# Self attention with its pieces in slots: output normalisation moved, layer norm transposes apart, free places ahead of the output projection

## What is computed

```python
h = _layernorm(x, ln1_g, ln1_b)
x = x + _mha(h, h, sa_wq, sa_bq, sa_wk, sa_bk, sa_wv, sa_bv, sa_wo, sa_bo)
# _mha: q, k, v = h @ w.T + b in 16 heads of 32
#       softmax(q k^T / sqrt(32)) v, then @ wo.T + bo
```

## Time and profile before

| | us |
|---|---|
| median of 3 runs | 3602.26 (3598.32 to 3602.65) |
| the profiled execution | 3601.64 |
| its span, first to last instruction | 3599.9 |
| mean granted TensorE clock | 0.956 of full speed |
| PE busy | 3274.8 (91%) |
| DVE, ACT, POOL busy | 1747.6, 1695.5, 1279.3 |

### The profile page before, as it was taken

One profiled execution on the slowest core, in us unless ns is written; L12 is line 12 of the kernel. 1 busy time (PEld: TensorE's weight loads), 2 busy tenths in 40 slices (PEclk: granted clock), 3 DMA queues, 4 the chain that ended last, 5 costly groups with the idle time before them and its releaser, 6 DMA issues. The chain is left out here.

```text
span 3599.9 us, 44121 instructions
## 1 busy us (share of the span) xinstructions
PE 3274.8 (91%) x15024; PEld 2629.4 (73%) x15024; DVE 1747.6 (49%) x2646; ACT 1695.5 (47%) x4068; POOL 1279.3 (36%) x1424
## 2 busy tenths in 40 slices
PE   4899979999999958999999999758999799999999
PEld 3788857888888745776666667447888678888887
DVE  3566644222222136787788777535666442222221
ACT  2676644222222216666666666526766442222222
POOL 2455431111111115666666666514554211111110
PEclk8999989999999968999999999879999899999999
DMA  3112113111111132334333433231121131111110
GB/s 97 37 58 78 63 65 106 47 47 48 47 47 47 51 119 68 92 105 112 101 103 104 115 95 98 65 109 46 51 75 63 65 103 36 36 36 36 36 36 36
DMA packets 170341, 249.76 MB, mean 69 GB/s; under 512 B 38710, under 2 KB 57350, under 8 KB 170118
## 3 DMA queue, kind: packets, MB, share of 16 engines
q1 hardware_dynamic: 170118, 246.94, 22.6%
HBM read 115.45 MB, written 50.33 MB: 46 GB/s over the span
## 5 line engine op out<-in xcount | busy, mean ns | idle before, releaser
L1008 DVE TENSOR_REDUCE L1sa_nmax<-L1sa_s 128x2 f32<-128x1024 f32 x256 | 310.4, 1213 | 201.3 <-PE L1sa_s L810 201.2
L1147 POOL TENSOR_TENSOR L1sa_El<-L1sa_E,L1sa_Eh 128x1024 fp32r<-128x1024 f32 x128 | 314.6, 2458 | 163.6 <-ACT L1sa_Eh L914 126.5
L440 DVE TENSOR_TENSOR L1ff_gl<-L1ff_gf,L1ff_gh 128x512 fp32r<-128x512 f32 x128 | 95.1, 743 | 471.9 <-ACT L1ff_gh L400 471.9
L440 DVE TENSOR_TENSOR L0ff_gl<-L0ff_gf,L0ff_gh 128x512 fp32r<-128x512 f32 x128 | 95.0, 742 | 440.1 <-ACT L0ff_gh L400 440.0
L923 ACT ACTIVATE L1sa_E<-L1sa_st 128x1024 f32<-128x1024 f32 x256 | 260.5, 1018 | 87.4 <-PE L1sa_st L826 42.2
L386 ACT ACTIVATE L0ff_gf<-L0ff_f,cols 128x512 f32<-128x512 f32 x128 | 88.3, 690 | 451.4 <-PE L0ff_f L94 451.4
L386 ACT ACTIVATE L1ff_gf<-L1ff_f,cols 128x512 f32<-128x512 f32 x128 | 88.3, 690 | 450.3 <-PE L1ff_f L94 450.3
L92 PE MATMUL L1ff_f<-L1ff_hTh,L1ff_Wh 128*128 128x512 f32 x512 | 203.1, 397 | 5.7 <-POOL L1ff_hTl L235 5.7
L92 PE MATMUL L0ff_f<-L0ff_hTh,L0ff_Wh 128*128 128x512 f32 x512 | 202.9, 396 | 5.7 <-POOL L0ff_hTl L235 5.7
L914 ACT ACTIVATE L1sa_Eh<-L1sa_E 128x1024 fp32r<-128x1024 f32 x192 | 200.6, 1045 | 0.2
L92 PE MATMUL L0ff_acc<-L0ff_Wh,L0ff_gh 128*128 128x512 f32 x512 | 199.4, 389 | 1.1 <-DVE L0ff_gl L440 1.1
(11 more groups left out here) (322 smaller groups left out, 9023.6 us busy)
## 6 DMA issues: line engine op xcount, KB each, us to landing
L1sa_OLN<-L1sa_osb SPq DMA_DIRECT2D x128, 192.0 KB, 2.6
L0ff_xs<-x SPq DMA_DIRECT2D x64, 256.0 KB, 3.8
L1sa_stack_q<-L1sa_parts_q SPq DMA_DIRECT2D x128, 128.0 KB, 2.6
L1sa_stack_k<-L1sa_parts_k SPq DMA_DIRECT2D x128, 128.0 KB, 2.6
L1ff_xs<-x SPq DMA_DIRECT2D x64, 256.0 KB, 3.5
L0ca_xs<-in_x SPq DMA_DIRECT2D x32, 256.0 KB, 4.0
L0ca_stage<-in_x SPq DMA_DIRECT2D x32, 256.0 KB, 3.3
x<-L0ca_stage SPq DMA_DIRECT2D x32, 256.0 KB, 2.1
```

Of the source, the lines that this page charges most:

```text
L440: nc.vector.tensor_tensor(gl[:, j % 2, :], gf[:, j % 2, :], f32(gh[:, j % 2, :]), ALU.subtract)\
L1008: nc.vector.reduce_max(nmax[:, h % 2, 2 * (n % 2):2 * (n % 2) + 2], s_bank[:, :, :], AX.X, negate=True)\
L1147: nc.gpsimd.tensor_tensor(El[:, n % 2, :], E[:, n % 2, :], f32(Eh[:, n % 2, :]), ALU.subtract)\
```

## The change

It all stands in `self_attention` and the tables ahead of it.

- The pieces stand in 73 slots instead of 68: four free ones (None) ahead of the output projection's first unit, one behind the first T. The T pieces are no longer in a row but stand between quarters of O 2 and O 3. The 73 slots are spread over the 64 halves. The first O quarter moves from half 1 of step 3 to half 0 of step 5.
- A bank is fixed by kind: q and T have bank 0, k bank 1, V alternates, O is on 0, 1, 1, 1. `before` gives the unit ahead on the same bank.
- `o_hi` is one instruction (bias and rounding together), and moves from the start of step 8g+11 (8g+17 where g mod 4 = 0) to behind the exponential of step 8g+12 (8g+18). `o_lo` adds the bias itself, with scalar_tensor_tensor, and moves to step 8g+13 (8g+19).
- ACT: in steps with n mod 8 = 4 `o_out` comes behind `exp`. POOL: `m_split` at the start of even steps, `o_sum` one step later, `o_scaled` behind it (one step later still where g mod 4 = 1), and `place_v` in even steps only, two in some. SP: the line-up of a group's first head one step later, stacks at computed steps, loads of x three steps later. DVE: statistics of the layer norm one to three steps later.

```diff
+SA_SLOTS = (quarters("q", 0, 2) + quarters("k", 0, 2) + [None] * 4 + quarters("O", -1, 0) + quarters("O", -1, 1)
+            + quarters("q", 0, 3) + quarters("k", 0, 3) + [("T", 1, 0, 0), None] + quarters("O", -1, 2, 0, 2)
+            + [("T", 1, 1, 0)] + quarters("O", -1, 2, 2, 4) + [("T", 1, 2, 0)] + quarters("O", -1, 3, 0, 2)
+            + [("T", 1, 3, 0)] + quarters("O", -1, 3, 2, 4) + quarters("q", 1, 0) + quarters("k", 1, 0)
+            + quarters("V", 1, 0) + quarters("V", 1, 1) + quarters("q", 1, 1) + quarters("k", 1, 1)
+            + quarters("V", 1, 2) + quarters("V", 1, 3))
...
+def sa_bank(kind, i):
+    return {"q": 0, "k": 1, "T": 0}.get(kind, i % 2 if kind == "V" or i < 2 else 1)
...
+        for i, quarter in enumerate(SA_SLOTS):
+            if quarter:
+                half = i * 2 * STEPS // len(SA_SLOTS)
+                halves[half].append(quarter)
+                ready[quarter[:3]] = half // 2 + half % 2
...
+        stack_steps = sorted((max(ready[n, ahead, g] + 1, 8 * (g + 4 * ahead) + 4 * pair - 14), n == "k", pair, ahead, g)
+                             for n, ahead, g in ready if n in "qk" for pair in range(2))
...
-                    if n % 2 == 0 and n >= 2:
+                    if n % 8 == 3 and n >= 3:
+                        line_up((n - 3) // 2)
+                    elif n % 2 == 0 and n % 8 != 2 and n >= 2:
                         line_up((n - 2) // 2)
...
-                    if s in (15, 16, 17, 18) and b + 2 < B:
-                        load(b + 2, s - 15)
-                    if b > 0 and s in (7, 9, 16, 18):
-                        store(b - 1, (7, 9, 16, 18).index(s))
+                    if s in (18, 19, 20, 21) and b + 2 < B:
+                        load(b + 2, s - 18)
+                    if b > 0 and s in (8, 9, 16, 19):
+                        store(b - 1, (8, 9, 16, 19).index(s))
...
-                nc.scalar.activation(onorm[:, :], onorm[:, :], ACT.Identity, bias=badj[:, 2, g % G:g % G + 1])\
-                    .then_inc(e_ob2.sem, e_ob2.unit)
-                act.wait_ge(e_ob2.sem, e_ob2.no(g))
-                nc.scalar.activation(oTh[:, g % G, :], onorm[:, :], ACT.Copy).then_inc(e_oh.sem, e_oh.unit)
+                add_hi(nc, oTh[:, g % G, :], onorm[:, :], badj[:, 2, g % G:g % G + 1]).then_inc(e_oh.sem, e_oh.unit)
...
-                    for g in range(GROUPS):
-                        if n == 8 * g + (17 if g % G == 0 else 11):
-                            o_hi(g)
-                    if n % 2 == 0 and n >= 2:
+                    if n % 2 == 0 and n % 8 != 4 and n >= 2:
                         o_out((n - 2) // 2)
                     if 0 <= n + 1 < PAIRS and EH_BY[(n + 1) % 8] == "act":
                         e_hi(n + 1)
                     if 0 <= n + LEAD_T < PAIRS:
                         exp(n + LEAD_T)
+                    if n % 8 == 4 and n >= 4:
+                        o_out((n - 2) // 2)
+                    for g in range(GROUPS):
+                        if n == 8 * g + (18 if g % G == 0 else 12):
+                            o_hi(g)
...
-                add_lo(nc, oTl[:, g % G, :], oTh[:, g % G, :], onorm[:, :], None).then_inc(e_ol.sem, e_ol.unit)
+                add_lo(nc, oTl[:, g % G, :], oTh[:, g % G, :], onorm[:, :], badj[:, 2, g % G:g % G + 1])\
+                    .then_inc(e_ol.sem, e_ol.unit)
...
-                        if n == 8 * g + (17 if g % G == 0 else 11):
+                        if n == 8 * g + (19 if g % G == 0 else 13):
                             o_lo(g)
...
-                        if s in (25, 27, 29, 31):
-                            normalise(b + 2, (s - 25) // 2)
+                        if s in (26, 28, 30, 31):
+                            normalise(b + 2, (26, 28, 30, 31).index(s))
...
-            PLACE = {1: 0, 2: 1, 3: 2, 4: 3, 5: 4, 6: 5, 7: 6}
+            PLACE = {1: 0, 2: 2, 3: 2, 4: 4, 5: 4, 6: 6, 7: 6}
...
+                    if n % 2 == 0 and 0 <= n + 6 < PAIRS:
+                        m_split((n + 6) // 2)
                     if n % 8 == 2 and n >= 10:
-                        o_scaled((n - 10) // 8)
+                        o_sum((n - 10) // 8)
+                    for g in range(GROUPS):
+                        if n == 8 * g + (11 if g % G == 1 else 10):
+                            o_scaled(g)
                     if 0 <= n + 1 < PAIRS and EH_BY[(n + 1) % 8] == "pool":
                         e_hi(n + 1)
-                    if n % 8 == 1 and n >= 9:
-                        o_sum((n - 9) // 8)
                     if 0 <= n + 1 < PAIRS and EL_BY[(n + 1) % 8] == "pool":
                         e_lo(n + 1)
-                    if n % 2 and 0 <= n + 7 < PAIRS:
-                        m_split((n + 7) // 2)
```

More of the change, by code:

```diff
@@ L549, in _, with quarters @@
                 body(b, b % 2, b == B - 1)
[L552 to L554 removed]
+def quarters(kind, ahead, i, first=0, end=4):
+    return [(kind, ahead, i, c) for c in range(first, end)]
+SA_SLOTS = (quarters("q", 0, 2) + quarters("k", 0, 2) + [None] * 4 + quarters("O", -1, 0) + quarters("O", -1, 1)
[4 more added lines that the diff above has]
+            + quarters("V", 1, 2) + quarters("V", 1, 3))
 SA_FIRST = [("T", c) for c in range(KT)] + [("q", 0), ("k", 0)] + [("V", t) for t in range(TT)] + [("q", 1), ("k", 1)]
 STEPS = H * 2
[L559 to L565 removed]
+def sa_bank(kind, i):
+    return {"q": 0, "k": 1, "T": 0}.get(kind, i % 2 if kind == "V" or i < 2 else 1)
 def self_attention(nc, name, cst, x_in, x_biased, x_out, ln_w, ln_b, wq, bq, wk, bkv, wv, wo):
@@ L607, in self_attention @@
         LEAD_S, LEAD_T = 8, 2
-        halves = sa_pieces()
-        ready = {u[:3]: half // 2 + half % 2 for half, quarters in enumerate(halves) for u in quarters}
+        halves = [[] for _ in range(2 * STEPS)]
+        ready = {}
+        for i, quarter in enumerate(SA_SLOTS):
[3 more added lines that the diff above has]
+                ready[quarter[:3]] = half // 2 + half % 2
         evacs = [[] for _ in range(PAIRS + 1)]
@@ L612, in self_attention @@
         for b in range(B):
-            for kind, ahead, i in SA_ORDER:
+            for kind, ahead, i in dict.fromkeys(q[:3] for q in SA_SLOTS if q):
                 if exists(b + ahead):
@@ L617, in self_attention @@
         units += [("O", B - 1, t) for t in range(TT)]
-        no = {u: i for i, u in enumerate(units)}
-        product_no = {u: i for i, u in enumerate(u for u in units if u[0] != "T")}
+        before = {}
+        for bank in range(2):
+            on_bank = [u for u in units if sa_bank(u[0], u[2]) == bank]
+            before.update(zip(on_bank[1:], on_bank))
+        finished = [(kind, 0, i) for kind, i in SA_FIRST if kind != "T"]
+        for b in range(B):
+            finished += [(k, b + a, i) for k, a, i, c in filter(None, SA_SLOTS) if c == KT - 1 and exists(b + a)]
+        finished += [("O", B - 1, t) for t in range(TT)]
+        stack_steps = sorted((max(ready[n, ahead, g] + 1, 8 * (g + 4 * ahead) + 4 * pair - 14), n == "k", pair, ahead, g)
+                             for n, ahead, g in ready if n in "qk" for pair in range(2))
+        product_no = {u: i for i, u in enumerate(finished)}
         e_lnb = ph.events("lnb_set", 2)
@@ L756, in bank_free @@
             def bank_free(u):
-                kind, b, i = units[u - 2]
+                kind, b, i = before[u]
                 if kind == "T":
@@ L767, in piece @@
             def piece(kind, b, i, c):
-                u = no[kind, b, i]
-                bank = pj[u % 2]
-                if c == 0 and u >= 2:
-                    bank_free(u)
+                bank = pj[sa_bank(kind, i)]
+                if c == 0 and (kind, b, i) in before:
+                    bank_free((kind, b, i))
                 if kind == "T":
@@ L1218, in _ @@
                             place_v(b, j)
-                    if s == 23 and b + 2 < B:
+                    if s == 25 and b + 2 < B:
                         rsqrt(b + 2)
```

32 lines of the change are left out of this document (11 added, 21 removed), and 5 rows, old and new, of the table s.

## The result

| | before | after |
|---|---|---|
| median of 4 runs each on one chip, us | 3602.31 (3598.32 to 3602.65) | 3676.74 (3674.18 to 3679.47) |
| ratio | | 1.0209 (95%: 1.0192 to 1.0227) |
| span of the profiled execution | 3599.9 | 3672.4 |
| mean granted clock | 0.956 | 0.952 |

What follows compares the result with a forecast made beforehand. PE was taken to bound the kernel, busy for 91% of the span. Batches 1 to 6 (+42), batch 7 (+3), batch 0 (-5) and the end (-0.7) gave +39 on 3601.6 us: 3641 us, range 3600 to 3660.

Steps and rivals of the forecast that it cites:

- Steps 4 and 5: Around the free places: PE waits 2.1 (exponential), 0.7 (maxima's copy) and 3.0 us (oTl), together 5.8 us a batch.
- Seven waits of 0.53: Maxima's transpose in steps 2, 8, 10, 16, 18, 24, 26: 0.53 us each, 3.7 us a batch, where these had 2.1.
- T, in steps 12, 15 and 17: T pieces apart: waits of 1.3, 1.2 and 2.1 us, 4.6 a batch, where the transposes waited 4.1.
- Step 20: Transpose waits 2.6 us, as group 1's scaling in step 19 waits for group 0's low part, behind a maximum.
- rival 1: Step 5: the low part is there when PE comes to the first O piece; 3566 us, chance 0.13.
- the lock: Step 5: POOL's El blocks DVE's low part, both reading SBUF; PE waits 3.0 us, without the rule 2.0.
- the sign that I named: In the trace: oTl at 2 us and more in most cases would show the lock forecast right.
- rival 3: PE under half busy for 9 us lowers the clock longer: +2 to 4 us a batch, 3655 to 3670, chance 0.12.
- The fixed banks add nothing else, since each predecessor is over a step ahead: Banks fixed by kind: no further waits claimed, except for O2 to O3.
- costed at nothing: SP's stacks and x loads move one to three steps: no cost claimed; if cover goes, scores wait 2.6 us.
- the term of step 28: One more layer norm operation precedes a maximum in step 28: a wait of 0.4 us where 0.5 was.
- batch 0 and batch 7: Batch 0, without O, was to win 5 us (bounds 0 and -8); batch 7, without T, to lose 3.

Runs made afterwards that it cites:

- olo_first: Kernel after, with DVE making the low part (o_lo) ahead of the maximum of its step: 3634.47 us (one run).
- fused_alone: Kernel before, with only the fused o_hi and the o_lo that adds the bias, at their old places: 3611.17 us, ratio 1.0027.
- ends: Kernel after, with T in the prologue and O of the last batch alternating between the two banks again: 3673.93 us (one run).
- t3_first: Kernel after, with T3's low part ahead of the reciprocal half on DVE in step 17: 3666.37 us (one run).
- all_mended: Kernel after, with low parts and O2's sum before maxima, T3 before reciprocal, alternating end banks, pair-0 stacks first, normalisation in even steps: 3602.23 us, ratio 1.0001.
- olo_oout_sum: Kernel before, with fused o_hi, biased o_lo ahead of the maximum, o_out behind exp in every even step, o_sum one step later: 3592.98 us, ratio 0.9968.
- before_oout: Kernel before, with o_out behind the exponential on ACT in every even step: 3620.97 us, ratio 1.0056.

## Why the prediction was right or wrong

**Right: the idle time of the full batches.** Predicted were 17.1 us a batch, the trace of batch 3 has 17.6; +42 for six batches, measured +45.2. Most terms agree singly. Steps 4 and 5: 5.8 predicted, 4.7 measured (2.1, 0.7 and 3.0 against 1.48, 0.42 and 2.83). Seven waits of 0.53: six of them, 3.2 instead of 3.7. T, in steps 12, 15 and 17: 1.3, 1.2 and 2.1 predicted, 0.94, 1.01 and 1.78 measured. Step 20: 2.6 and 2.56. olo_first supports the order on DVE as the cause of the largest, and of the one in step 20, and it was the point from which rival 1 decided: the first O product waited behind a maximum of its own step. The swap removes that and gives back 42 us; on top of the fused instruction alone it gives 32. Rival 1's price doesn't follow, though. It had 3566 us for a low part that is there in time; with a wait of 0.2 us for it olo_first has 3634, since the other new waits stay.

**Right, but not as a sign: the lock.** The bounds 0.67 and a blocked low part were the right ones: fused_alone shows the new form at 2.54 us. In step 5 I reckoned POOL's El from 1.0 us into the step, and the low part from 2.3 to 3.9; the trace has 0.98, and 2.37 to 3.87. So it was held for 0.8 us of its 1.50, as forecast. But a low part of 1.6 us in the forecast's own working doesn't go with the sign that I named, oTl at 2 us and more in most cases. None of the 32 in after reaches 2 us, their mean is 1.02, and that sign failed. In the kernel before 19 of 32 are over 2 us. The wait was made by the place behind the maximum first, and by the lock second.

**Wrong: "Total +39" has no term for the clock.** Busy time grew by 14.1 us in six batches for the same products. The text had it only in the upper bound ("another 1.7 us a batch at half clock") and in rival 3. Measured are 2.3 us a batch: after the wait of step 5 the clock is at 0.50 for 6.83 us. This is the largest term that the sum lacks, 14 of the 33 us between +39 and the 72.5 of the spans. The idle time of the full batches was forecast well, and rival 3's clock came beside it, not in its place; with the other misses the time is above rival 3's 3655 to 3670 as well.

**Wrong: "The fixed banks add nothing else, since each predecessor is over a step ahead".** That was reasoned for the loop. In the prologue four T units follow each other on one bank, and at the end O1, O2 and O3 do. With the end's -0.7 for the fused instruction there should have been a gain; measured are +4.4 and +3.9, and ends gives 4.5 and 3.2 of them back.

**Wrong: SP's order, "costed at nothing".** "The first user of a stack set is some steps behind" holds for the pair issued first. The k stacks of pair 0 are issued behind q's pair 1, and the stack lands late for step 24: 1.0 us, and 0.5 in step 25. Also the term of step 28 (0.4) is 1.43 and a new 0.43 stands in step 0, both behind maxima that normalisations delay. These took 1.96 us in step 27 and 2.37 in step 30, both begun behind POOL's El, against 0.53 without it. The same section of the Trainium skill (SBUF — State Buffer, Who interferes with whom) lists tensor_scalar among the instructions that can contend with GpSimd for the port, and the two durations agree; I had applied it to the low part alone.

**Wrong: batch 0 and batch 7.** Batch 0 was to win 5 us and lost 0.6; its idle time went from 13.2 to 16.0. Its trace has 3.2 us for hTl in step 17 and 2.6 us for the exponential in step 20, the waits that I had counted for the full batches and forgotten here. t3_first halves the first of them (1.6 us) and makes batch 0 2.5 us shorter than in after; in all_mended batch 0 takes 114.26 us, 5.0 less than before the change, which is the gain that was forecast. Batch 7 lost 5.4 instead of 3.

In one line, of 72.5 us: 45 are idle time of the full batches (42 forecast, term by term), 14 are clock, 8 the two ends, 6 the first and last batch, and -1 what follows the stage. The 33 us that the forecast lacks are 14 of clock, 9 at the ends, 6 in batch 0, 3 of idle time in the full batches and 2 in batch 7, less that 1.

## What to carry to other kernels

On an engine with a fixed order, look at what stands directly ahead of an instruction that PE waits for. A maximum of scores just issued ahead of a low part whose inputs were ready cost 42 us in the changed kernel (one run) and 32 beside the fused instruction alone, and no other edit tried weighed as much. Making an instruction shorter, or giving PE free places, need not help: the shorter one let POOL start first and lock DVE (+9 us), and the free places emptied PE while the chain from El to the transpose ran on (+14 us). When waits are added up, give the clock a term of its own, and follow a new assignment of buffers through the prologue and the end as well as through the loop.

## What the hardware showed that was not expected

A scalar_tensor_tensor with both inputs in SBUF takes 0.93 us when it starts ahead of POOL's tensor_tensor (0.74 at the least, in after) and 2.54 us when it starts 0.35 us behind it. A tensor_scalar that started 0.31 us behind the same POOL instruction took 2.37 us instead of 0.53, and POOL's kept its 2.40: only the second comer lost. POOL lost where DVE's tensor_tensor was the first, 3.35 to 3.38 us.

The clock does not follow the sum of idle time alone. In all_mended and in olo_first batch 3 has 10.2 and 13.1 us idle at a granted 1.00, in fused_alone 10.1 us at 0.96, in olo_oout_sum 8.1 us at 0.97. The two at 1.00 have no single wait over 1.8 us, fused_alone one of 2.9 and olo_oout_sum two of 2.1 and 2.3. But the kernel before has 2.1 and 2.0 at 0.99, and before_oout 2.6, 2.3 and 2.1 at 0.99, so the longest wait isn't all of it either; what decides stays open.
